# Heads of Q and K laid side by side in DRAM, and the rows of a quad loaded in eight DMAs

## What is computed

```python
xn = layernorm(x)
# branch 1: attention with 16 heads of 16 features, causal, with a linear decay
Q, K, V = xn @ q_w.T + q_b, xn @ k_w.T + k_b, xn @ v_w.T + v_b
S[h, i, j] = K[h, i] . Q[h, j] / 4              # rows are keys, columns are queries
S = where(i < j, -inf, S) - (i - j)
s = (softmax(S, axis=-1) @ V) @ o_w.T + o_b
# branch 2: 8 experts, the two best of each token
h = gelu(xn @ fc1_w[e] + fc1_b[e]);  y = (h @ fc2_w[e] + fc2_b[e]) * alpha[e] * share[e]
g = silu(sum of the two y)
out = x + s * g
```

## Time and profile before

| | before |
|---|---|
| median of 3 runs | 722.7 us (719.65 to 725.21) |
| the profiled execution | 723.35 us |
| its span, first to last instruction | 721.5 us |
| mean granted TensorE clock | 0.981 |
| PE busy | 682.4 us (95%) |
| DVE, ACT, POOL busy | 535.4, 485.1, 231.4 us |
| moved by DMA | 124.46 MB, of which the 192 loads of rows 25.2 MB |

### The profile page before, as it was taken

One profiled execution on the slowest core, in us unless ns is written; L12 is line 12 of the kernel. 1 busy time (PEld: TensorE's weight loads), 2 busy tenths in 40 slices (PEclk: granted clock), 3 DMA queues, 4 the chain that ended last, 5 costly groups with the idle time before them and its releaser, 6 DMA issues.

```text
span 721.5 us, 17539 instructions
## 1 busy us (share of the span) xinstructions
PE 682.4 (95%) x6042; PEld 462.0 (64%) x6042; DVE 535.4 (74%) x1146; ACT 485.1 (67%) x994; POOL 231.4 (32%) x330
## 2 busy tenths in 40 slices
PE   6976999999999999999999999999789999999976
PEld 3865776565555556556555655654359888999764
DVE  6535987999989989998998999896224554444298
ACT  3542443677777877788787777878776666666374
POOL 5331110134023323423342432300034757576300
PEclk9997999899999999999999999999999999999998
DMA  6999966333765685487568657710359686865396
GB/s 194 267 251 308 350 215 198 96 57 74 127 128 138 140 178 148 120 173 159 137 139 171 142 141 149 169 25 19 94 132 251 244 206 216 223 189 177 112 401 245
DMA packets 77207, 124.46 MB, mean 172 GB/s; under 512 B 14184, under 2 KB 47464, under 8 KB 77000
## 3 DMA queue, kind: packets, MB, share of 16 engines
q1 hardware_dynamic: 68368, 98.32, 54.4%
q0 software_dynamic: 8752, 25.02, 10.8%
HBM read 72.56 MB, written 49.72 MB: 169 GB/s over the span
## 4 chain that ended last, share of the span: by engine, by line
PE 82%; DVE 8%; DMA 6%; ACT 2%; issue 2%; POOL 1%; SPq 0%; DVEq 0%; POOLq 0%; ACTq 0%
PE ps L1578 20%; PE ps L1511 14%; PE ps L1562 13%; PE ps L1667 8%; PE ps L1689 8%; PE ps L1500 7%; PE ps L1460 5%; PE ps L1470 3%; DMA arena<-in_x 2%; DMA arena<-xs_dram 2%; PE ps L1650 2%; DVE mxa L1103 2%; DVE arena L1412 1%; DVE x_room L1417 1%; DVE arena L1402 1%
## 5 line engine op out<-in xcount | busy, mean ns | idle before, releaser
L1103 DVE TENSOR_REDUCE mxa<-ps 128x1 f32<-128x512 f32 (+3 forms) x608 | 357.9, 653 | 35.2 <-PE ps L1500 20.3
L967 ACT ACTIVATE arena<-ps 128x512 f32<-128x512 f32 x576 | 304.0, 603 | 82.3 <-PE ps L1562 41.1
L1511 PE MATMUL ps<-aug 57*128 57x512 f32 (+3 forms) x768 | 218.4, 401 | 2.1 <-DVE mxa L1103 0.3
L1562 PE MATMUL ps<-aug 59*128 59x512 f32 (+3 forms) x768 | 216.0, 399 | 0.5 <-ACT arena L967 0.5
L1578 PE MATMUL ps<-arena,v_q 128*32 128x512 f32 (+3 forms) x1536 | 154.9, 498 | 6.7 <-ACT arena L967 6.3
L1562 PEld LDWEIGHTS ps<-aug 59*128 59x128 f32 x768 | 109.9, 186 | 76.2 <-ACT arena L967 69.0
L1511 PEld LDWEIGHTS ps<-aug 57*128 57x128 f32 x768 | 109.6, 186 | 37.2 <-DVE mxa L1103 23.4
L889 POOL DMA_INDIRECT y_dram<-arena,y_row_of x71 | 69.4, 978 | 54.2 <-DVE y_row_of L1341 47.3
L862 POOL DMA_INDIRECT xs_dram<-arena,slot x64 | 62.6, 978 | 74.1 <-ACT arena L967 70.5
L1500 PE MATMUL ps<-key_mask,key_rows 64*128 64x64 bf16 (+2 forms) x704 | 79.0, 208 | 0.0
L1667 PE MATMUL ps<-arena 128*128 128x128 f32 x568 | 75.2, 275 | 0.0
(11 more groups left out here) (148 smaller groups left out, 639.3 us busy)
## 6 DMA issues: line engine op xcount, KB each, us to landing
aug<-k_parts SPq DMA_DIRECT2D x96, 128.0 KB
aug<-q_parts SPq DMA_DIRECT2D x96, 128.0 KB
arena<-xs_dram SPq DMA_DIRECT2D x71, 128.5 KB, 2.6
k_parts<-arena SPq DMA_DIRECT2D x16, 512.0 KB, 5.9
q_parts<-arena SPq DMA_DIRECT2D x16, 512.0 KB, 5.9
arena<-y_dram SPq DMA_DIRECT2D x16, 512.0 KB, 6.7
xn_dram<-arena SPq DMA_DIRECT2D x8, 512.0 KB, 6.9
a_dram<-arena SPq DMA_DIRECT2D x128, 32.0 KB
```

The costliest lines, as they stand in the source:

```text
L967: nc.scalar.activation(prob_slot(q, i), score_bank(q, i), ACT.Exp).then_inc(exp_done, 1)
L1103: nc.vector.tensor_reduce(dst, src, AX.X, ALU.max).then_inc(piece_used, 1)
L1511: ins = nc.tensor.matmul(banks[:, at_ * width:(at_ + 1) * width], k_aug[n][rows, hp, ib * P:(ib + 1) * P], q_aug[n][rows, hp, lo:lo + widt ...
L1562: ins = nc.tensor.matmul(out_[:, col0:col0 + hi - lo], q_aug[n][rows, h // SIDES_OF_ARRAY, jb * P:(jb + 1) * P], k_aug[n][rows, h // SIDES ...
```

## The change

Within a quad the columns of the weights of K and Q are permuted while they are split (`by_head` reads, `by_side` writes), so that a row of `k_parts` and `q_parts` is no longer (head pair, side, feature) but (side, feature, head pair): the two heads that share a partition lie in neighbouring DRAM rows, and a partition takes one run of 8 KB. Each split of K and Q weights becomes two instructions of 128 x 256 (`HP` = 2) on ACT, DVE and POOL. The biases are permuted by loading each in two DMAs to every other partition. `K_PART` becomes (1, 0, 0) and `Q_PART` (0, 0, 1), so that the two stacks with the high part are neighbours: one load fills both, with a source that names the same 16 rows twice (an outermost dimension of step 0 and count 2). A quad now has eight loads, in the order of `LOADS`: four of the high part into 32 partitions (256 KB), then four of the low part into 16 partitions (128 KB); the bytes stay 1.5 MB. `PACE` becomes 3 and `STORE_BESIDE` 5. The products that are summed are the same, in another order.

```diff
--- before.py
+++ after.py
@@ -28,8 +28,8 @@
 
 
 
-K_PART = (0, 0, 1)
-Q_PART = (0, 1, 0)
+K_PART = (1, 0, 0)
+Q_PART = (0, 0, 1)
 NSPLIT = 2
 NBIAS = 3
 DATA_ROWS = len(K_PART) * HD
@@ -114,9 +114,10 @@
 ROUTE_FROM = 3
 AHEAD = 14
 AHEAD_OF_MAXIMA = 4
-PACE = 2
-STORE_BESIDE = 8
-NLOAD = 2 * SIDES_OF_ARRAY * len(K_PART)
+PACE = 3
+STORE_BESIDE = 5
+LOADS = [(part, side, of_array) for part in range(NSPLIT) for side in range(2) for of_array in range(SIDES_OF_ARRAY)]
+NLOAD = len(LOADS)
 
 
 def stream(ahead, more=2):
@@ -171,8 +172,9 @@
 FIRST_BANK = (6, 3)
 ZERO_TILES = E
 
-KEY_WEIGHTS = ("wk", "kb")
-WEIGHTS = ("wq", "qb", "wv", "gate")
+WEIGHTS = ("wq", "wv", "gate")
+NKEY = 1 + HP
+NWEIGHT = len(WEIGHTS) + HP
 CONSTS = ("later", "sooner", "ones_row", "ones_col")
 LATE_CONSTS = ("num", "before", "alpha", "wo", "ob", "vb")
 NCONST = SIDES_OF_ARRAY * len(CONSTS) + len(LATE_CONSTS)
@@ -378,6 +380,15 @@
 
         wk_two = [in_split(KT * D * s, D) for s in range(2)]
         wq_two = [in_split(KT * D * (2 + s), D) for s in range(2)]
+
+        def by_head(w, j):
+
+            return w.rearrange("p k (q j f) -> p (k q) j f", j=HP, q=NQ // B)[:, :, j, :].rearrange("p e (r d) -> p e r d", d=HD)
+
+        def by_side(w, j):
+
+            return w.rearrange("p k (q r d j) -> p (k q) r d j", j=HP, r=SIDES_OF_ARRAY, d=HD)[:, :, :, :, j]
+
         wvg_two = [in_split(KT * (4 * D + (D + E) * s), D + E) for s in range(2)]
         xnT_high, xnT_low = [[in_split(KT * (4 * D + 2 * (D + E)) + KT * BANK * (CHUNKS * s + c), BANK) for c in range(CHUNKS)]
                              for s in range(2)]
@@ -506,15 +517,21 @@
             sp.sem_inc(x_in[0], 16)
             sp.dma_start(idf[:, :], ident_f).then_inc(ident_in, 16)
             loads = {"wk": (wk_sb[:, :, :], weights(wkT)), "wq": (wq_sb[:, :, :], weights(wqT)),
-                     "qb": (qb_sb[:, :], qb), "kb": (kb_sb[:, :], kb), "vb": (vb_sb[:, :], vb),
+                     "vb": (vb_sb[:, :], vb),
                      "wv": (wvg_sb[:, :, 0:D], weights(wvT)), "gate": (wvg_sb[:, :, D:D + E], weights(gate)),
                      "before": (before_sb[:, :], before),
                      "num": (num_sb[:, :], numbers), "alpha": (alpha_sb[:, :], alpha),
                      "wo": (wo_sb[:, :, :], weights(woT)), "ob": (ob_sb[:, :], ob)}
-            for name in KEY_WEIGHTS:
-                sp.dma_start(*loads[name]).then_inc(key_in, 16)
+
+            def load_bias(to, of, loaded):
+                for j in range(HP):
+                    sp.dma_start(to[j:P:HP, :], of.rearrange("(q j f) m -> j q f m", j=HP, q=P // QF)[j]).then_inc(loaded, 16)
+
+            sp.dma_start(*loads["wk"]).then_inc(key_in, 16)
+            load_bias(kb_sb, kb, key_in)
             for name in WEIGHTS:
                 sp.dma_start(*loads[name]).then_inc(weights_in, 16)
+            load_bias(qb_sb, qb, weights_in)
             load_x_chunk(0, 1)
 
             def store_normalised(i, b, c):
@@ -552,11 +569,14 @@
             load_x_chunk(1, 0)
             store_normalised(0, 0, 0)
             def load_rows(q, n, g):
-                part, side, of_array = g // (2 * SIDES_OF_ARRAY), g // SIDES_OF_ARRAY % 2, g % SIDES_OF_ARRAY
+                part, side, of_array = LOADS[g]
                 aug, src, parts_ = ((k_aug, k_parts, K_PART), (q_aug, q_parts, Q_PART))[side]
-                first = ROW_TILE * of_array + HD * part
-                heads = src[parts_[part], bass.ts(q, QF), :].rearrange("(j r d) t -> r d j t", r=SIDES_OF_ARRAY, d=HD)
-                sp.dma_start(aug[n][first:first + HD, :, :].bitcast(fp32), heads[of_array]).then_inc(aug_in[n], 16)
+                at_ = [p for p in range(len(parts_)) if parts_[p] == part]
+                first = ROW_TILE * of_array + HD * at_[0]
+                heads = src[part, bass.ts(q, QF), :].rearrange("(r d j) t -> r d (j t)", r=SIDES_OF_ARRAY, d=HD)[of_array]
+                heads = bass.AP(heads.tensor, heads.offset, [[0, len(at_)]] + [list(x) for x in heads.ap])
+                rows = aug[n][first:first + len(at_) * HD, :, :].rearrange("p j t -> p (j t)").bitcast(fp32)
+                sp.dma_start(rows, heads).then_inc(aug_in[n], 16)
 
             def load_maxima(q, n):
                 sp.wait_ge(mT_ready, q + 1)
@@ -731,10 +751,14 @@
             for n in range(AUG):
                 nc.gpsimd.memset(v_q[n][:, :, :, HD:2 * HD], 1.0).then_inc(ones_set, 1)
 
-            pool.wait_ge(weights_in, 16 * len(WEIGHTS))
-            for n, (w, two) in enumerate(((wvg_sb, wvg_two), (wq_sb, wq_two))):
-                pool.wait_ge(weights_high, n + 2)
-                nc.gpsimd.tensor_tensor(two[1], w[:, :, :], two[0].bitcast(fp32), ALU.subtract).then_inc(weights_low, 1)
+            pool.wait_ge(weights_in, 16 * NWEIGHT)
+            pool.wait_ge(weights_high, 2)
+            nc.gpsimd.tensor_tensor(wvg_two[1], wvg_sb[:, :, :], wvg_two[0].bitcast(fp32), ALU.subtract).then_inc(weights_low, 1)
+            pool.wait_ge(weights_high, 3)
+            for j in range(HP):
+                ins = nc.gpsimd.tensor_tensor(by_side(wq_two[1], j), by_head(wq_sb, j), by_side(wq_two[0], j).bitcast(fp32),
+                                              ALU.subtract)
+            ins.then_inc(weights_low, 1)
 
             def load_decays(n):
                 for side in range(SIDES_OF_ARRAY):
@@ -937,12 +961,16 @@
 
             roots(0)
             normalise_first()
-            act.wait_ge(key_in, 16 * len(KEY_WEIGHTS))
-            nc.scalar.activation(wk_two[0], wk_sb[:, :, :], ACT.Identity, scale=SCALE).then_inc(weights_high, 1)
+            act.wait_ge(key_in, 16 * NKEY)
+            for j in range(HP):
+                ins = nc.scalar.activation(by_side(wk_two[0], j), by_head(wk_sb, j), ACT.Identity, scale=SCALE)
+            ins.then_inc(weights_high, 1)
             take_transposed(0, 0, 0)
-            act.wait_ge(weights_in, 16 * len(WEIGHTS))
+            act.wait_ge(weights_in, 16 * NWEIGHT)
             nc.scalar.activation(wvg_two[0], wvg_sb[:, :, :], ACT.Copy).then_inc(weights_high, 1)
-            nc.scalar.activation(wq_two[0], wq_sb[:, :, :], ACT.Copy).then_inc(weights_high, 1)
+            for j in range(HP):
+                ins = nc.scalar.activation(by_side(wq_two[0], j), by_head(wq_sb, j), ACT.Copy)
+            ins.then_inc(weights_high, 1)
             act.wait_ge(bias_ready, 1)
             roots(1)
             for b in range(B):
@@ -1152,11 +1180,13 @@
                 ins = nc.vector.tensor_scalar(xnb[0][:, t, :], xb[0][:, t, :], rstd[:, 0, t:t + 1], shift[:, 0, t:t + 1],
                                               ALU.mult, ALU.add)
             ins.then_inc(xn_half, 1)
-            dve.wait_ge(key_in, 16 * len(KEY_WEIGHTS))
+            dve.wait_ge(key_in, 16 * NKEY)
             nc.vector.tensor_scalar(kbs_sb[:, :], kb_sb[:, :], SCALE, None, ALU.mult).then_inc(bias_ready, 1)
             dve.wait_ge(weights_high, 1)
-            nc.vector.scalar_tensor_tensor(wk_two[1], wk_sb[:, :, :], SCALE, wk_two[0].bitcast(fp32),
-                                           ALU.mult, ALU.subtract).then_inc(wk_low, 1)
+            for j in range(HP):
+                ins = nc.vector.scalar_tensor_tensor(by_side(wk_two[1], j), by_head(wk_sb, j), SCALE,
+                                                     by_side(wk_two[0], j).bitcast(fp32), ALU.mult, ALU.subtract)
+            ins.then_inc(wk_low, 1)
             dve.wait_ge(xpose_done, 4)
             dve.wait_ge(xT_ready, 1)
             nc.vector.tensor_copy(xnT_high[0][:, 1, :], bank(FIRST_BANK[1])).then_inc(xT_ready, 1)
@@ -1539,7 +1569,7 @@
                     send_counts(s, banks)
                 else:
                     if piece == 0:
-                        pe.wait_ge(aug_in[(n + d) % AUG], 192 * ((q + d) // AUG) + 192)
+                        pe.wait_ge(aug_in[(n + d) % AUG], 16 * NLOAD * ((q + d) // AUG + 1))
                     send_piece((n + d) % AUG, s, banks, piece)
 
             def half_unit(q, n, i):
```

## The result

| | before | after |
|---|---|---|
| median, runs of one chip | 721.6 us | 985.6 us |
| ratio | | 1.363 (95% interval 1.357 to 1.369) |
| span of the profiled execution | 721.5 us | 983.6 us |
| mean granted TensorE clock | 0.981 | 0.852 |
| start of window 0 | 124.7 us | 161.7 us |

The forecast was 938 us, between 850 and 1035.

What follows compares the result with a forecast made beforehand. PE was taken to set the pace in the steady windows, DMAs in the prologue. 723.35 us + 196 (15.1 us in each of 13 windows) + 18 (prologue) + 0.5 (startup) = 938 us, range 850 to 1035.

Steps and rivals of the forecast that it cites:

- The mechanism: Loads of K and Q rows: a 256 KB load with two copies outermost runs on two engines; forecast's chance 0.79.
- The deadline: Windows 1 to 13: 14.8 us from first load to PE's first use; any lateness lengthens PE's period, PE standing 12.1 us.
- the expert weights ahead: Windows: in about two of three, 512 KB of weights queue ahead of the first load, 0.7 us on average.
- the stretch behind it at the lower clock: Windows, after PE's stop: 4.5 us of work run at 1.2 GHz, 2.3 us more.
- the time of a quad's loads: Windows: 26.9 us from first issue to last landing, of which 20.9 for four 256 KB loads at 25.1 GB/s an engine.
- the prologue: Before window 0: 13 us from the load of x behind quad 0's rows, 5 for quads 1 and 2; 18 us.
- the step for quads 1 and 2: Prologue: stores behind these rows are needed some 25 us later and nearly fit; 5 us for both, between 0 and 42.
- All 16 engines: Rival for the row loads: copies don't steer the split, no loss; about 717 us, 711 to 724; chance 0.11.
- Hidden: Rival for the windows: two engines, but loads land within 14.8 us; prologue alone pays, 741 us; chance 0.03.
- Slow engines at 14 GB/s: Rival: two slow engines, four loads take 37 us, a window grows by 31 us; 1175 us total; chance 0.07.
- The tail: End of the kernel: stays as it is, as do windows 0, 14 and 15.
- The start: Startup: splits in two instructions and two more bias DMAs cost 0.5 us, between nothing and 1.5 us.

Runs made afterwards that it cites:

- the half dose: Changed kernel with two-copy loads kept for K's high part only, Q's high part by four 16-partition loads: 884.5 us against 740.2 for the kernel before, ratio 1.194.

## Why the prediction was right, and where its terms were off

**The mechanism.** A 256 KB load with the copies outermost runs on two engines: counted (eight small packets for four loads, in one window and over the whole execution), and told apart by putting the same repetition inside (1.000, beside 1.194 with it outermost) and by taking it out (1.003). The prediction had worked this out from counts for 1 and for 16; that a DMA is cut alike on both sides was an assumption there, and the count bears it out.

**The deadline.** 14.8 us of room, 13 late windows, the stream behind the wait taken in order: 13 waits of 14.2 us, and windows of 42.6 us on average, where 40.1 had been worked out. Of the 16.8 us that window q = 3 grew by, 14.0 are the wait of PE (forecast 12.1, or 12.8 with the expert weights ahead), 2.3 the stretch behind it at the lower clock (forecast 2.3; the granted clock of 0.80 over these 12.5 us gives 2.5), and 0.5 PE's stream up to the wait, which the forecast had at nothing.

**The term that was too small: the time of a quad's loads.** 29.4 us against 26.9 in window q = 3; the 13 windows together grow by 226 us (17.4 us each on average) instead of 196. The rate of the two engines was right when they are undisturbed (25.1 GB/s each used, 26 measured), and 23 in the changed kernel between 289.2 and 303.5 us, with POOL's queue beside them. What I had as free is the time in which the narrow loads and the wide ones are in flight together; the half dose shows that a packet then takes 0.8 us instead of 0.31. Whether this makes the 2.5 us isn't shown: the two engines' packets can't be told apart there, and turning the order round saved nothing in the windows. How the 2.5 us are shared between the narrow loads, the stores and POOL's traffic stays open.

**The term that was half: the prologue.** 37.0 us (36.6 when tried alone) instead of 18. The load of x landed at 74.4 us against 70: 17 us later than before where 13 were forecast. What failed is the step for quads 1 and 2, "their 21 us nearly fit: I take 5 us for both, between 0 and 42 us"; they cost about 20. Of these, 15.2 us are the stop before window 0. The step looked at the stores behind the rows and at the reuse of their buffers, and left out the maxima of quad 0, which are loaded behind the rows of quad 2: eight of their 64 pieces waited on the two engines, and PE waited for them. The prediction had seen this wait for the windows ("so that `m_in` isn't late a second time") and not for the prologue. The rest, some 4 us, isn't traced to one cause: the store behind the rows of quad 1 took 19.4 us to land, and SP's own issues were held (6.2 and 7.8 us above). The stated 0 to 42 us held it, but for another reason than the one that was given.

**The rivals.** All 16 engines: excluded by the count. Hidden: excluded, PE waits 13 times. Slow engines at 14 GB/s: excluded by 53 GB/s for two, though the mean rate with many in flight, 10 to 11 GB/s an engine, shows that this price wasn't out of reach; it was seen only while 8 or more engines were busy with loads of rows.

**What stayed as it was.** The tail takes 189.6 us from 794 us on, as the 189.5 us from 532 us on before. The start: forecast 0.5 us; its own run gave 3 us in the median with nothing in the trace to hold it.

## What to carry to other kernels

Before a DMA is changed in shape, count what stands outermost in its source and its destination: two copies put there dealt the transfer out to two engines in these runs, eight rows to eight, and the same bytes with 16 rows outermost run on 16. A small load that is queued behind such a transfer is late with it, even if only a few of its pieces fall on the same engines. A hidden transfer has a number, the room between its issue and its first use; a shape that makes it longer than that is paid in every window, and again in the clock. Merging DMAs saves issues on a queue that didn't bind here, so even the best form of it gained nothing.

## What the runs showed of the hardware

The same wide load of 32 rows had two small packets with two copies outermost and 16 with 16 rows outermost. Two engines, with 8 KB packets to 32 partitions, moved 53 GB/s; eight engines writing to 8 partitions a load moved 89; sixteen writing to 16 partitions a load 145 to 163. Four or eight times the engines gave less than twice or about three times the rate, with fewer partitions a load; which of the two sets the rate wasn't separated. In the prologue SP was held while the two engines were behind: a single DMA issue took up to 6.2 us, so that what stood behind it was issued later too.
